# Two stacked attention operands stored ready-made in DRAM, their loads merged and reordered, and the matmuls of maxima on eight PSUM banks, eight ahead

## The reference

```python
logits = jnp.einsum('bhqd,bhkd->bhqk', Q, K) / scale
logits = logits * scale_matrix
attn = jax.nn.softmax(logits, axis=-1)
out = jnp.einsum('bhqk,bhkd->bhqd', attn, V) * (1.0 + yellow * eps_adaptive)
```

## Time and profile before

| | us |
|---|---|
| median of 3 runs | 3189.24 |
| lowest and highest run | 3179.98, 3189.51 |
| the profiled execution's own time | 3191.58 |
| its span, first to last instruction | 3189.8 |
| TensorE's mean granted clock in it | 0.851 of full |
| busy PE / DVE / ACT / POOL | 2359.1 / 1927.5 / 1410.9 / 495.9 |
| DMA | 58.91 MB, mean 18 GB/s |

### The profile page before, as it was taken

The page is one execution under the profiler, slowest core; times in us unless marked ns, Lnnn a source line. Parts: engine busy times, 40 slices in busy tenths (PEclk is TensorE's granted clock), DMA queues, the critical chain, the costliest instruction groups (busy, mean ns, idle before and its releaser), DMA issues.

```text
span 3189.8 us, 46714 instructions
## 1 busy us (share of the span) xinstructions
PE 2359.1 (74%) x17632; PEld 1338.3 (42%) x17632; DVE 1927.5 (60%) x4063; ACT 1410.9 (44%) x2529; POOL 495.9 (16%) x308
## 2 busy tenths in 40 slices
PE   5699388577689758857768947867766993886676
PEld 5467122254547512235545731225453671222545
DVE  5725587555553579565653449956565255885556
ACT  1133177364424327644622415746261341773644
POOL 0123000213022200030203310003211230002130
PEclk9999599778889869968779977987877995997788
DMA  3000200101000010010100010000000002001010
GB/s 126 1 1 1 61 5 9 24 9 25 18 1 1 9 53 5 12 25 8 23 17 1 1 45 18 9 14 21 22 16 8 1 1 60 5 9 24 9 25 17
DMA packets 50744, 58.91 MB, mean 18 GB/s; under 512 B 19458, under 2 KB 31106, under 8 KB 49988
## 3 DMA queue, kind: packets, MB, share of 16 engines
q1 hardware_dynamic: 50500, 55.70, 6.8%
HBM read 25.25 MB, written 8.66 MB: 11 GB/s over the span
## 4 chain that ended last, share of the span: by engine, by line
PE 44%; DVE 22%; ACT 11%; issue 9%; DMA 5%; SPq 5%; POOL 4%; DVEq 0%; ACTq 0%; POOLq 0%
PE PS L1085 39%; DVE arena L920 8%; ACT arena L575 5%; DMA tmp<-xf 3%; ACT arena L530 2%; POOL arena L384 2%; PE PS L1347 2%; PE PS L1103 1%; DVE s_at L976 1%; SPq L333 1%; DMA tmp<-tmp 1%; DVE tmp L945 1%; POOL arena L417 1%; SPq L334 1%; PE PS L1159 1%
## 5 line engine op out<-in xcount | busy, mean ns | idle before, releaser
L1085 PE MATMUL PS<-arena 128*32 128x256 f32 (+4 forms) x10240 | 824.4, 355 | 243.8 <-DMA arena<-scr 85.1
L920 DVE TENSOR_REDUCE arena<-PS 128x1 f32<-128x512 f32 x1024 | 646.9, 684 | 124.6 <-PE PS L1085 124.0
L1085 PEld LDWEIGHTS PS<-arena 128*32 128x32 f32 (+4 forms) x10240 | 312.6, 124 | 754.4 <-DVE arena L920 304.9
L530 ACT ACTIVATE arena<-PS 128x1024 f32<-128x1024 f32 x512 | 516.9, 1032 | 155.7 <-PE PS L1085 154.9
L867 DVE TENSOR_TENSOR arena<-PS,arena 128x512 f32<-128x512 f32 x128 | 86.1, 688 | 323.6 <-PE PS L1085 302.1
L1085 PE MATMUL PS<-wqkv,arena 128*128 128x512 f32 x384 | 221.7, 732 | 65.4 <-ACT arena L561 56.2
L1085 PEld LDWEIGHTS PS<-w2e,arena 128*128 128x128 f32 x2048 | 246.1, 192 | 53.7 <-issue 51.7
L498 ACT ACTIVATE arena<-PS 128x512 f32<-128x512 f32 x256 | 150.8, 597 | 247.6 <-PE PS L1085 247.5
L1085 PE MATMUL PS<-w2e,arena 128*128 128x128 f32 x2048 | 246.7, 275 | 0.0
L575 ACT ACTIVATE arena<-PS,arena 128x128 f32<-128x128 f32 x512 | 229.8, 521 | 15.9 <-DVE arena L1028 15.9
L560 ACT ACTIVATE arena<-PS 128x1024 f32<-128x1024 f32 x64 | 65.6, 1024 | 324.3 <-DVE s_at L976 247.8
(11 more groups left out here) (259 smaller groups left out, 3430.4 us busy)
## 6 DMA issues: line engine op xcount, KB each, us to landing
arena<-arena SPq DMA_DIRECT2D x120, 128.0 KB, 2.2
arena<-scr_q SPq DMA_DIRECT2D x192, 32.0 KB
arena<-scr_k SPq DMA_DIRECT2D x192, 32.0 KB
scr_q<-arena SPq DMA_DIRECT2D x12, 256.0 KB, 2.8
scr_k<-arena SPq DMA_DIRECT2D x12, 256.0 KB, 3.1
x_in<-in_x SPq DMA_DIRECT2D x5, 512.0 KB, 3.8
xT<-tmp SPq DMA_DIRECT2D x64, 32.0 KB
tmp<-tmp SPq DMA_DIRECT2D x64, 32.0 KB
```

The source lines that it names most:

```text
L530: act.activation(pb[:, n % 8], pair(2 * (n % 2)), ACT.Exp).then_inc(S["p"], 1)
L920: dve.tensor_reduce(mxp[:, h % 2, j, t, hf:hf + 1], PS[:, ring_bank("mx", h, n), :], AX, ALU.max)\
L1085: return pe.matmul(o, w, v, start=start, stop=stop, **kw)
```

## The change

Both stacks are stored ready-made: each piece goes to DRAM as often as it stands in the stack (12 stores in place of 6), four of them (piece 1) issued by ACT, eight by SP. The two rows of ones lie behind the K stack in DRAM once and for all: 16 small stores ahead of the batch loop in place of one. A group is read with four DMAs (48 or 50 rows each) in place of 26; of group 0, ACT issues two. SP loads groups 0 and 1 first, group 2 behind `load_max(0)` and group 3 behind `load_max(2)`. The first 32 tiles of maxima go round all eight PSUM banks, the others round banks 5 to 7 as before. AHEAD falls from 44 to 40.

```diff
-PARTS_W = 6
-Q_STACK = (0, 0, 0, 1, 1, 2)
-K_STACK = ((0, 3), (3, 2), (5, 1))
+PARTS_W = 12
+Q_STACK = ((0, 1, 2), (3, 4), (5,))
+K_STACK = ((0, 3, 5), (1, 4), (2,))
-AHEAD = MPH + 12
+AHEAD = MPH + 8
...
-            return 5 + ring_at[kind, h, n] % 3
+            i = ring_at[kind, h, n]
+            return i % 8 if i < MPH else 5 + i % 3
+
+        ring_last, bank_user = [], {}
+        for i, v in enumerate(ring):
+            ring_last.append(bank_user.get(ring_bank(*v)))
+            bank_user[ring_bank(*v)] = v
+
+        def stack_of(v, g, r):
+
+            return v[GH * g:GH * g + GH].rearrange("(s r) i n -> r i s n", r=2)[r]
...
-            sp.dma_start(d["scr_1"], one_f[0:PIECES_M]).then_inc(S0["one_w"], 16)
-            sp.wait_ge(S0["one_w"], 16)
+            for h in range(H1):
+                sp.dma_start(d["scr_k"][h, STACK:STACK + PIECES_M], one_f[0:PIECES_M, 0]).then_inc(S0["one_w"], 16)
+            sp.wait_ge(S0["one_w"], 16 * H1)
...
-                for qk in range(2):
-                    for i in range(3):
+                for i in (0, 2):
+                    for qk in range(2):
                         sp.wait_ge(S["bf%d" % (i + 1)], qk + 1)
-                        sp.dma_start((scr_k if qk else scr_q)[:, i], qk3[:, qk, i, :]).then_inc(S["scr_w"], 16)
+                        for slot in (K_STACK if qk else Q_STACK)[i]:
+                            sp.dma_start((scr_k if qk else scr_q)[:, DK * slot:DK * slot + DK], qk3[:, qk, i, :])\
+                                .then_inc(S["scr_w"], 16)
                 sp.wait_ge(S["scr_w"], 16 * PARTS_W)
...
+                    for r in range(2 if g else 1):
+                        sp.dma_start(QS[64 * r:64 * r + STACK, g], stack_of(scr_q, g, r)).then_inc(S["qs_loaded%d" % g], 16)
+                        sp.dma_start(KS[64 * r:64 * r + STACK + PIECES_M, g], stack_of(scr_k, g, r))\
+                            .then_inc(S["qs_loaded%d" % g], 16)
...
-                for g in range(NGRP):
-                    load_group(g)
+                load_group(0)
+                load_group(1)
                 for h in range(HALVES):
                     load_max(h)
+                    if h in (0, 2):
+                        load_group(2 + h // 2)
...
                     act.copy(qk3[:, qk, 1], qkr[:, qk]).then_inc(S["bf2"], 1)
+                for qk in range(2):
+                    act.wait_ge(S["bf2"], qk + 1)
+                    for slot in (K_STACK if qk else Q_STACK)[1]:
+                        act.dma_start(d["scr_k" if qk else "scr_q"][:, DK * slot:DK * slot + DK], qk3[:, qk, 1, :])\
+                            .then_inc(S["scr_w"], 16)
                 act.wait_ge(S["scr_w"], 16 * PARTS_W)
+                act.dma_start(QS[64:64 + STACK, 0], stack_of(d["scr_q"], 0, 1)).then_inc(S["qs_loaded0"], 16)
+                act.dma_start(KS[64:64 + STACK + PIECES_M, 0], stack_of(d["scr_k"], 0, 1)).then_inc(S["qs_loaded0"], 16)
...
-                    if i >= 3:
-                        kind, h, n = ring[i - 3]
+                    if ring_last[i]:
+                        kind, h, n = ring_last[i]
...
-                            pe.wait_ge(S["qs_loaded%d" % g], 16 * 2 * (6 + 6 + 1))
+                            pe.wait_ge(S["qs_loaded%d" % g], 16 * 4)
```

More of the change, by code:

```diff
@@ L614, in _ @@
             dve.wait_ge(S0["k_loaded"], 48)
-            dve.wait_ge(S0["one_w"], 16)
+            dve.wait_ge(S0["one_w"], 16 * H1)
             k0 = [1]
@@ L1570 @@
         d[name] = nc.dram_tensor(f"in_{name}", v.shape, mybir.dt.from_np(v.dtype), kind="ExternalInput").ap()
-    d["scr_q"] = nc.dram_tensor("scr_q", (H1, 3, DK, N), BF16, kind="Internal").ap()
-    d["scr_k"] = nc.dram_tensor("scr_k", (H1, 3, DK, N), BF16, kind="Internal").ap()
+    d["scr_q"] = nc.dram_tensor("scr_q", (H1, STACK, N), BF16, kind="Internal").ap()
+    d["scr_k"] = nc.dram_tensor("scr_k", (H1, STACK + PIECES_M, N), BF16, kind="Internal").ap()
     d["scr_m"] = nc.dram_tensor("scr_m", (2, PIECES_M, GH * HALF), BF16, kind="Internal").ap()
-    d["scr_1"] = nc.dram_tensor("scr_1", (PIECES_M, 2 * N), BF16, kind="Internal").ap()
     out = nc.dram_tensor("out_x", (B, N, W), F32, kind="ExternalOutput").ap()
```

## The result

| | before | after |
|---|---|---|
| median of 4 runs, same chip, us | 3188.57 | 3222.03 |
| lowest and highest | 3179.98, 3189.51 | 3219.11, 3222.91 |
| profiled execution's span | 3189.8 | 3219.6 |
| mean granted clock | 0.851 | 0.85 |

The ratio is 1.0104, interval 1.0086 to 1.0122: 33 us slower, a little more than 1% and clear of the noise, where 3180 was forecast and 3158 to 3203 was the range. One run of the kernel before, taken beside experiments 9 to 12, was a slow one of 5530.85 us and is left out of their ratios.

What follows compares the result with a forecast made beforehand. PE, DVE and DMA waits share the chain, so no engine bounds the whole. Gains 11.4 less losses 9.0 make 2.4 a batch, 9.6 in four, less 0.5: profiled 3191.6 becomes 3182.5, median 3180; range 3158 to 3203 us.

Steps and rivals of the forecast that it cites:

- Stores and loads: Before the first maxima tile: ready-made stacks and fewer loads start tiles near 1124.5 instead of 1130.88, gain 6.4 a batch.
- Eight banks: First 32 maxima tiles: sixteen pairs at 1.26 us in place of 1.46, gain 3.0 a batch.
- The row waits: Main loop, halves 1 to 6: PE waits 1.1 us each for the row of maxima at AHEAD 40.
- The late rows: Halves 1 and 3: rows now 1.3 to 1.8 us late were expected on time, instruction packets having passed.
- The copies: ACT's copy of bank 4 comes 3.0 us late in two halves a batch, adding losses of 0.8 and 3.8.
- The end: After the last maxima tile: two steps fewer, 1.85 us, less 0.25 for a late move_out(2), gain 1.6 a batch.
- Rival B: Main loop: the clock falls at the row waits, 1.4 us each in halves 1, 2, 4 and 6; 3202; chance 0.2.
- Rival A: Main loop: the row of maxima is in time, copy waits stay, gain 6.8 a batch; 3162; chance 0.2.
- D: Before the first tile: stores don't keep the rate, so the 6.4 gain is 3.6; 3191; C and D 0.15.
- C: Halves 1 and 3: instruction packets stay, rows 1.3 and 1.8 later, 3.1 a batch; 3192; C and D 0.15.
- the first tile at 14.6 us: Sign for the gains: first maxima tile some 14.6 us after SP's first store, 21 before.
- rows of 1.34 in all halves: Sign that instruction packets have passed: each row of maxima is loaded 1.34 us after its store, in all halves.

Runs made afterwards that it cites:

- experiment 9: Experiment 6 with each piece stored once (six stores) and the stacks made by ten loads per row half: 3136.54 us against 3189.65 for the kernel before, ratio 0.9829.
- experiment 10: Experiment 6 with AHEAD 42 in place of 44: 3150.51 us, ratio 0.9872 to the kernel before.
- experiment 11: Kernel before with two output buffers for bank 4's copies alone: 3166.14 us, ratio 0.9927 to the kernel before.
- experiment 12: Experiment 6 with all four loads of group 0 issued by SP: 3145.05 us, ratio 0.9860 to the kernel before.
- experiment 1: Changed kernel with only AHEAD taken back to 44: 3167.74 us against 3187.65 for the kernel before, ratio 0.9936.
- experiment 2: Kernel before with AHEAD 40 alone: 3241.17 us, ratio 1.0164 to the kernel before.
- experiment 4: Experiment 1 with group 1 loaded behind the first row of maxima: 3162.77 us, ratio 0.9913 to the kernel before.
- experiment 7: Experiment 4 with each 50-row K load cut in 48 rows and 2 rows: 3161.23 us, ratio 0.9911 to the kernel before.
- experiment 8: Experiment 4 with all twelve stores issued by SP, none by ACT: 3163.61 us, ratio 0.9920 to the kernel before.
- experiment 5: Changed kernel (AHEAD 40) with two buffers for bank 4's copies: 3182.03 us, ratio 0.9986 to the kernel before.
- experiment 6: Experiment 4 (AHEAD 44, group 1 late) with two output buffers for bank 4's copies: 3139.50 us, ratio 0.9856 to the kernel before.

## Why the prediction was wrong

The losses were looked for in the right place: with two steps less, the row of maxima and the copies come too late. What failed was the sum, and so the sign: it had gains of 11.4 and losses of 9.0 a batch, and by the table they were 6.4 (stores and loads 2.4, banks 3.8, half 1 0.2) and 12.7. Three steps failed: the rate of group 0's loads, the lateness of rows 1 and 6, and the end.

Experiments 1 and 2 cut the error in another way. By the forecast's own terms the shorter lead cost 9.0 - 2.0 = 7.0 a batch, 28 us, and all the rest won 9.4 a batch, 38. Measured, the lead costs 54 and the rest wins 20. So the lead is the larger half of the error.

- **Stores and loads, the largest single term: 6.4 forecast, 2.4 measured.** The step was "Group 0 is 785 KB: 2.2 us at 364 GB/s, plus 1.7". The loads took 6.8 in the second batch. Of the 2.9 too much, group 1 costs 1.2 in the mean (experiment 4), and the rest is a rate well under that of the earlier trace rows: 264, 227, 229 and 234 GB/s in the four us from 1132 on. In experiment 4, without group 1, the bytes take some 3.5 us in place of 2.2, and the time ahead of them and behind them is the forecast's 1.7. Ten engines for the K loads explain little of it: with those loads cut the bytes still take 3.3 (experiment 7). Why the rest is slow stays open. The end of the range given for this, 3.6, had group 1's bytes in it but at the full rate. The stores took 11.7 for 10.7: the DMA engines moved 236 and 279 GB/s in the two us from 1123 on and 363 to 385 only later. That the second queue gives nothing was right (experiment 8).
- **Eight banks: 3.0 forecast, 3.8 measured.** DVE makes 32 tiles in 19.26, 1.20 a pair, faster than the 1.26 that the earlier trace rows show in the main loop.
- **The row waits: 1.1 forecast, 1.0 to 1.1 measured** where the row comes as usual (halves 3 and 5 of the changed kernel, halves 2, 3 and 5 of experiment 2). This step holds to a tenth of a microsecond, and the slack of 1.4 from which it came is borne out by experiments 10 and 11.
- **The late rows.** "PE will be two steps further in its program at T0, so I expect these packets to have passed by then" was half right. Before, rows 1 and 3 are late by 1.2 us or more in every batch. In experiment 2 neither is; in the changed kernel row 1 is in two batches of four, and row 3 is late by 0.4 to 0.5 in two. But row 6 is late in all eight batches of these two:

```profile
1307.89 0.31 SPq L324 DMA_DIRECT2D scr_m<-arena  x1
1310.49 1.29 SPq L329 DMA_DIRECT2D arena<-scr_m  x2
```

Its load is issued 2.60 after its store, not 1.34, PE waits 2.4, and steps of 1.47 and 1.98 follow at a lower clock (granted 0.78 and 0.73 on the mean of the two stretches, 1.00 before):

```profile
1311.00:1312.00 1.00, 0.00 (x0) 0.00 (x0) 1.00 (x2) 0.00 (x0) 0.00 (x0) 1.00 0.01 3
1312.00:1316.00 4.00, 2.80 (x22) 0.57 (x23) 1.44 (x3) 1.92 (x2) 0.00 (x0) 0.78 0.01 1
1316.00:1319.00 3.00, 2.72 (x28) 0.63 (x24) 2.03 (x4) 2.04 (x4) 0.00 (x0) 0.73 0.00 0
```

Half 7 loses 3.4 in place of 1.1, half 2, where row 1 is still late in two batches of four, 2.5 in place of 1.1: 3.7 in sum. The clock falls behind six of the eight waits longer than 1.5 us. Behind the other two, of 2.60 and 2.56, it stays at 1.00, and the half loses just its wait. The packets do go with the late rows: in six of the traces (before, after, experiments 2, 5, 6 and 10) all 39 rows that are late by 1.2 us or more have a packet of the instruction queue q8 in the 2.6 us behind their store, and 4 of the other 153 rows have one. Whether the packet causes the delay, and whether it keeps its place in PE's program, is argued from this and from the shift to row 6, not tested.
- **The copies: +0.8 and +3.8 forecast, +0.4 and +4.3 measured.** The second is right, and the copies' share was tested by taking the wait away (experiments 5, 6 and 11). The first is right in part by luck. The copy waits 2.04 and 1.94 in half 4 of two batches, but only 0.66 and 0.55 in the other two, where PE had already waited 1.56 and 1.51 for row 3 and ran behind it at a granted clock of 0.53 and 0.54. That half loses 3.7 and 3.6 all the same.
- **The end: 1.6 won forecast, 0 measured.** The third group's copy was put at 0.25. In two batches of four it waits 1.3. Of these two lines the first, with 2.04, is the copy in half 6, and the second, with 1.26, is that of the end:

```profile
1290.57 0.58 ACT L549 COPY tmp<-PS 128x512 f32<-128x512 f32 x1 [2.04 <-DMA tmp<-tmp]
...
1341.00 0.58 ACT L549 COPY tmp<-PS 128x512 f32<-128x512 f32 x1 [1.26 <-DMA tmp<-tmp]
```

Steps at a lower clock follow it, and these two batches end in 27.96 and 26.73. The other two have no such wait and end in 25.40 and 25.30. A second thing moves this stretch: behind the last fold PE stands still for 1.9 us, and the clock falls to 0.50 for 3 to 7 us. Where it is low for the longest, the kernel before ends in 26.99 and 26.95, and the changed one, without the copy's wait, in 25.40 and 25.30: there the 1.6 of the forecast is won. In experiment 6 the clock stays at 1.00 in three batches, which end in 24.37, and falls in one, which ends in 27.03. The forecast didn't look at this fall. Experiment 5, without the copy's wait, ends in 24.2.

The errors add up: 4.0 for the loads, 3.7 for late rows, 1.6 for the end, 0.3 for the head and the copies, less 0.8 for the banks, are 8.8, and 2.4 won became 6.3 lost, 25 us in four batches where the spans differ by 30. Rival B had the sign and a part of the cause: the clock does fall, but at late rows and at copies. Behind the sixteen row waits of 0.90 to 1.16 us in the changed kernel it never did (the two short ones of experiment 5 are the exceptions). Rival A is out: 24 row waits at 40, ten at 42 and next to none at 44, as the computed slack has it. D came true by more than its price, and C's packets partly stayed with row 1 and otherwise moved to row 6. The range failed because each rival was priced alone, on the forecast's sum: B, D and a part of C were true together. Of the prediction's own signs, the first tile at 14.6 us, rows of 1.34 in all halves and undisturbed halves near 22.9 didn't all come (halves 2 and 7 are over 24); PE's waits of about 1 us and the two halves near 26 did.

## What to carry to other kernels

A software lead, the number of steps by which one engine runs ahead of another, is sized by the slowest chain that must fit in it, its disturbed case included: here the slack was 1.4 us, a step is 1.26, and cutting two steps cost 54 us where the steps saved were worth 8 by the forecast's terms. Where a buffer's reuse waits for a move, a second buffer (23 us) was worth more than all of the rearranged stores and loads (10 us, 14 with group 1 late). Merging loads saves issue time, but where nothing else runs the bytes that are stored twice to allow it are paid too: here they cost 3.1 us a batch and the merging saved 1.9.

## What the hardware showed that I had not expected

- Some of the small stores of the row complete 1.2 to 1.9 us late, mostly at the same rows of a given program, and each of the 39 found in six traces has a packet of the instruction queue beside it, as in the earlier trace rows. Shortening PE's lead by two steps moved them from rows 1 and 3 to row 6 (experiment 2). That the packet is the cause wasn't tested.
- A wait of PE costs more than itself: behind the 2.04 us wait of a copy, steps take 1.98 and more in place of 1.26 until the clock is back, so that half 4 of the second batch lost 4.5 in all, its row's wait of 1.0 included. The loss differs from batch to batch: behind two row waits of 2.6 the clock didn't fall.
- Reductions of PSUM tiles on DVE run at 0.60 us each while PE does only maxima, and at 0.63 in the main loop.
- Two stores of 256 KB took 3.25 us to issue on ACT while SP's were in flight too, where three took SP 1.90 before: the price of an issue isn't fixed here.
